# Layer 3 of a four-layer network: the head of the next chunk moved beside this chunk's stages, and local attention divided behind the context product

## The reference

```python
# between layers: x = x + s * g,  g = silu(ffn of the layer before);  xn = layernorm(x)
# L3 attention (16 heads of 8)
g = sigmoid(xn @ Wg + bg)                       # one gate a token
res = (1 - Z_I) * max(1 - Z_I - Z_J, 0) + Z_I * min(1 - Z_I + Z_J, 1)
scope = clip((s - 2) ** (1 - g) + 2 - |i - j|, 1e-32, 1)
probs = softmax(q k' / sqrt(8) + log(max(res * scope, 1e-32)))
s = probs @ v
# L3 feed-forward: two sub-layers (DEPTH = 2), each
#   local attention (8 heads of 64, windows of 64 looking one window back),
#   x = x + o @ wo;  then layer norm, w1, a * gelu(g), w2, x = x + ...
```

## Time and profile before

| | |
|---|---|
| median of three runs | 4228.34 us (4226.57 to 4237.04) |
| profiled execution, its own time | 4234.82 us |
| its span, first to last instruction | 4233.2 us |
| mean granted TensorE clock | 0.826 |
| busy: PE, PEld | 3121.1 us (74%), 1694.0 (40%) |
| busy: DVE, ACT, POOL | 2419.7 (57%), 1756.8 (42%), 1192.0 (28%) |

### The profile page before, as it was taken

One profiled execution on the slowest core, in us unless ns is written; L12 is line 12 of the kernel. 1 busy time (PEld: TensorE's weight loads), 2 busy tenths in 40 slices (PEclk: granted clock), 3 DMA queues, 4 the chain that ended last, 5 costly groups with the idle time before them and its releaser, 6 DMA issues. The chain is left out here.

```text
span 4233.2 us, 54691 instructions
## 1 busy us (share of the span) xinstructions
PE 3121.1 (74%) x20450; PEld 1694.0 (40%) x20450; DVE 2419.7 (57%) x3405; ACT 1756.8 (42%) x3556; POOL 1192.0 (28%) x878
## 2 busy tenths in 40 slices
PE   6788888887343778888767678676786867768687
PEld 3444444444131333444334344343443434434344
DVE  2344444444263778778855665556665565656655
ACT  2333333333132555556434434344343444535344
POOL 0000000000232454445543243332433324233242
PEclk7888888888655889999878879688796887969779
DMA  2000000000121222333300000000000000000001
GB/s 95 8 7 5 3 7 7 7 7 5 65 92 50 69 74 75 92 88 88 84 18 6 9 1 6 8 6 9 1 6 8 6 9 1 6 8 6 8 1 8
DMA packets 82171, 112.05 MB, mean 26 GB/s; under 512 B 9920, under 2 KB 47296, under 8 KB 81344
## 3 DMA queue, kind: packets, MB, share of 16 engines
q1 hardware_dynamic: 76608, 98.31, 7.7%
q0 software_dynamic: 5376, 11.02, 1.1%
HBM read 82.55 MB, written 26.74 MB: 26 GB/s over the span
## 5 line engine op out<-in xcount | busy, mean ns | idle before, releaser
L370 ACT ACTIVATE l_PT<-PB 128x512 f32<-128x512 f32 x512 | 277.9, 595 | 542.0 <-PE PB L281 542.0
L281 PE MATMUL PB<-l_QM,l_KP 32*128 32x256 f32 x2048 | 375.0, 496 | 131.6 <-DVE l_QM L419 76.0
L1412 POOL TENSOR_TENSOR l_ST<-l_ST,l_CT 128x1024 f32<-128x1024 f32 x128 | 316.4, 2472 | 354.3 <-DVE l_ST L1351 354.3
L408 DVE TENSOR_REDUCE keep_MXP<-PB 128x4 f32<-128x1024 f32 x256 | 301.3, 1219 | 109.1 <-PE PB L254 109.1
L1351 DVE TENSOR_TENSOR_SCAN l_ST<-l_DA,l_DB 128x1024 f32<-128x1024 f32 x128 | 355.6, 2778 | 4.4
L281 PEld LDWEIGHTS PB<-l_QM,l_KP 32*128 32x128 f32 x2048 | 242.7, 244 | 258.7 <-ACT l_PT L370 98.6
L704 POOL MEMSET l_KV<- 128x4 f32 x8 | 0.8, 104 | 941.3 <-POOLq L109 941.3
L1563 POOL TENSOR_TENSOR l_PT<-l_PT,l_PEN 128x512 f32<-128x512 f32 x168 | 213.1, 1290 | 186.0 <-ACT l_PT L370 186.0
L1345 DVE TENSOR_TENSOR l_DB<-PB,l_BT 128x1024 f32<-128x1024 f32 x128 | 155.3, 1213 | 137.5 <-PE PB L1111 137.5
L1274 ACT ACTIVATE l_DA<-PB,keep_aneg 128x510 f32<-128x510 f32 x256 | 161.1, 683 | 160.2 <-DVE l_ST L1351 83.4
L295 PE MATMUL PB<-l_PT,keep_VT 128*32 128x256 f32 x2048 | 187.6, 529 | 35.5 <-POOL l_PT L1563 25.6
(11 more groups left out here) (419 smaller groups left out, 6771.5 us busy)
## 6 DMA issues: line engine op xcount, KB each, us to landing
l_WB<-in_w2f_dram SPq DMA_DIRECT2D x80, 320.0 KB, 3.0
l_WB<-in_w2f_dram SPq DMA_DIRECT2D x80, 258.0 KB, 2.7
l_XR<-xs_mid SPq DMA_DIRECT2D x80, 64.0 KB, 1.8
ys_mid<-l_YO SPq DMA_DIRECT2D x80, 64.0 KB, 2.8
s_mid<-keep_S SPq DMA_DIRECT2D x17, 256.0 KB, 2.0
w3fs<-in_w3f_dram SPq DMA_DIRECT2D x1, 3127.0 KB, 18.1
keep_XI<-in_x_dram SPq DMA_DIRECT2D x9, 256.0 KB, 3.1
x_mid<-keep_X SPq DMA_DIRECT2D x9, 256.0 KB, 3.1
```

Of the source, the lines that this page charges most:

```text
L281: last = nc.tensor.matmul(PB[:, 4 + u % STBANKS, kt * SEQ:(kt + 1) * SEQ], b.KP[rows, a, i, k0:k0 + 128], b.QM[rows, n % 2, :], start=True ...
L370: nc.scalar.activation(b.PT[:, u % PSLOTS].rearrange("p k q -> p (k q)"), PB[:, 4 + u % STBANKS, :], ACT.Exp).then_inc(s.exp_done, 1)
L408: nc.vector.tensor_reduce(dst[:, 2 * pair:2 * pair + 2, :, 16 + n % 2], PB[:, 2 * pair:2 * pair + 2, :].rearrange("p r (t k) -> p r t k", ...
L1412: nc.gpsimd.tensor_tensor(b.ST[:, g % RING], b.ST[:, g % RING], b.CT[:, k % 2, :].unsqueeze(1).broadcast_to([128, 2, T]), ALU.mult).then_i ...
```

## The change

It does six things.

1. The head of a chunk's attention stage is done during the chunk before. Mixing (`gate_tokens`, now on POOL), turn, gate, residual, layer norm and gate logits run inside the attention stage, handed to PE, ScalarE and VectorE through a new argument `ahead`; the gate functions and the penalties run inside `layer3_ffn`, ten penalty steps and eight products on VectorE. Both penalty halves are VectorE's, written with other operations of the same value.
2. A new Block, `layer3_prepare`, does all of that once for the first chunk, in series, with the gather for the second.
3. Batch 0's multiplication by the penalties is shared like the others (three tiles on POOL).
4. In local attention the probabilities are no longer scaled. PE forms the row totals with two products by ones, and VectorE takes a reciprocal of 128x256 and multiplies the context by it. The loop is one step shorter; `G` and `HH` lie in the tile `CS`.
5. Loads, places and the two padding tiles reach one chunk further; the loads are issued at the start of `layer3_ffn`.
6. `att_tensor` issues `FIRST_MAX` = 11 fillers behind the first scores when there is no `ahead` (layer 0), and `NEXT_MAX` = 6 in layer 3. The two groups of fillers in layer 3's head go.

The diff, cut to its core:

```diff
+FIRST_MAX = 11
+NEXT_MAX = 6
+NEXT_TOKENS = 6
-def keep_warm(nc, c, PB, count=WARM):
+def keep_warm(nc, c, PB, count=WARM, bank=7):
@@ att_tensor
     scores(0)
+    if ahead:
+        ahead(0)
+    else:
+        keep_warm(nc, c, PB, FIRST_MAX)
...
             totals(0)
             if beside:
                 beside(0)
+            if ahead:
+                ahead(1)
...
+    if ahead:
+        ahead(2)
     values(BATCHES // 2 - 1)
     totals(1)
+    if ahead:
+        ahead(3)
@@ att_vector
-        for r in range(NR) if n == 0 else (NR - 1,):
+        u = NR * n + NR - 1
-        if masked and n == 0:
-            before(1)
-            weigh(0)
@@ layer 3, new functions
+def gate_products(nc, h, sq, link):
+    gates = slice(sq * SEQ, (sq + 1) * SEQ)
+    for t in (2 * sq, 2 * sq + 1):
+        nc.vector.scalar_tensor_tensor(out=h.T2[:, t, :], in0=h.AJ[:, gates], scalar=h.GI[:, t:t + 1], in1=h.GA[:, gates],
+                                       op0=ALU.add, op1=ALU.mult)
+        last = nc.vector.scalar_tensor_tensor(out=h.T1[:, t, :], in0=h.AJ[:, gates], scalar=h.NI[:, t:t + 1], in1=h.AJ[:, gates],
+                                              op0=ALU.add, op1=ALU.mult)
+    link(last)
...
+def penalty(nc, c, h, k, link):
+    sq, step = divmod(k, 5)
+    both, gates = slice(2 * sq, 2 * sq + 2), slice(sq * SEQ, (sq + 1) * SEQ)
+    two = lambda x: x[:, gates].unsqueeze(1).broadcast_to([128, 2, SEQ])
+    pen, t1, t2 = h.PEN[:, both], h.T1[:, both], h.T2[:, both]
+    if step == 0:
+        link(nc.vector.tensor_tensor(pen, c.dist.rearrange("p (t q) -> p t q", q=SEQ), two(h.PJ), ALU.add))
+    elif step == 1:
+        link(nc.vector.tensor_tensor(t2, t2, two(h.GA), ALU.min))
+    elif step == 2:
+        link(nc.vector.scalar_tensor_tensor(out=t1, in0=t1, scalar=0.0, in1=t2, op0=ALU.max, op1=ALU.add))
+    elif step == 3:
+        link(nc.vector.scalar_tensor_tensor(out=pen, in0=pen, scalar=1.0, in1=t1, op0=ALU.min, op1=ALU.mult))
+    else:
+        link(nc.vector.tensor_scalar(pen, pen, 1e-32, None, ALU.max))
@@ layer3_attention, PE
-                pe.wait_ge(s.y_mixed, 1)
...
-                keep_warm(nc, c, PB)
-                pe.wait_ge(s.x_gated, 1)
-                ln_tensor(nc, pe, s, c, c.X[:], PB)
-                keep_warm(nc, c, PB)
...
-                att_project(nc, pe, s, c, w, PB)
+                att_project(nc, pe, s, c._replace(XN=h.XN), w, PB)
+                def ahead(part):
+                    if part == 0:
+                        pe.wait_ge(s.y_gated, 1)
+                        turn_tokens(nc, c, PB, 7).then_inc(s.yT_ready, 1)
+                        pe.wait_ge(s.v_copied, 1)
+                        keep_warm(nc, c, PB, NEXT_MAX, 4)
+                        pe.wait_ge(s.y_copied, 1)
+                    elif part == 1:
+                        pe.wait_ge(s.x_ready, 1)
+                        nc.tensor.matmul(PB[:, 2, :], c.centre, h.X[:], start=True, stop=True).then_inc(s.ln_centred, 1)
+                    elif part == 2:
+                        pe.wait_ge(s.ln_square, 1)
+                        nc.tensor.matmul(PB[:, 3, :], c.mean, c.lnsq[:], start=True, stop=True).then_inc(s.ln_var, 1)
+                    else:
+                        pe.wait_ge(s.xn_ready, 1)
+                        ahead_gates(nc, h, w, PB).then_inc(s.gate_ready, 1)
@@ layer3_attention, ACT
+                def ahead(n):
+                    if n == 0:
+                        act.wait_ge(s.y_copied, 1)
+                        nc.scalar.activation(c.ga[:], c.Y[:], ACT.Abs).then_inc(s.ga_abs, 1)
+                    elif n == 1:
+                        act.wait_ge(s.ga_abs, 1)
+                        nc.scalar.activation(c.ga[:], c.ga[:], ACT.Exp, scale=-1.0).then_inc(s.ga_exp, 1)
+                    elif n == 2:
+                        act.wait_ge(s.ga_exp, 1)
+                        nc.scalar.activation(c.ga[:], c.ga[:], ACT.Ln, bias=c.one).then_inc(s.gate_log, 1)
+                    elif n == 4:
+                        act.wait_ge(s.gate_arg, 1)
+                        nc.scalar.activation(c.gb[:], c.gb[:], ACT.Exp).then_inc(s.gate_sigmoid, 1)
+                    elif n == BATCHES - 1:
+                        act.wait_ge(s.ln_centred, 1)
+                        nc.scalar.activation(c.lnsq[:], PB[:, 2, :], ACT.Square).then_inc(s.ln_square, 1)
+                    elif n == BATCHES:
+                        ahead_rstd(nc, act, s, c, PB)
@@ layer3_attention, DVE
+                def ahead(n):
+                    if n == 3:
+                        dve.wait_ge(s.gate_log, 1)
+                        nc.vector.scalar_tensor_tensor(out=c.gb[:], in0=c.Y[:], scalar=0.0, in1=c.ga[:], op0=ALU.min,
+                                                       op1=ALU.subtract).then_inc(s.gate_arg, 1)
+                    elif n == BATCHES:
+                        dve.wait_ge(s.kept, 2)
+                        ahead_norm(nc, dve, s, c, h, PB, link)
+                    elif n == BATCHES + 1:
+                        dve.wait_ge(s.gate_ready, 1)
+                        take_gates(nc, h, w, PB)
@@ layer3_attention, POOL
+                gate_tokens(nc.gpsimd, c, r, it + 1, link).then_inc(s.y_gated, 1)
+                nc.gpsimd.tensor_copy(c.X[:], h.X[:]).then_inc(s.kept, 1)
+                nc.gpsimd.tensor_copy(c.XN[:], h.XN[:]).then_inc(s.kept, 1)
+                pool.wait_ge(s.y_copied, 1)
+                nc.gpsimd.tensor_tensor(c.lnc[:], c.SI0[:], c.Y[:], ALU.mult).then_inc(s.product, 1)
+                for n in range(BATCHES):
+                    if n == NEXT_TOKENS:
+                        link(nc.gpsimd.tensor_tensor(c.lnc[:], c.lnc[:], c.gb[:], ALU.mult))
+                        pool.wait_ge(s.kept, 2)
+                        nc.gpsimd.tensor_tensor(h.X[:], c.X1[:], c.lnc[:], ALU.add).then_inc(s.x_ready, 1)
@@ layer3_ffn, PE
-                    for m in range(A + 4):
+                    for m in range(A + 3):
-                            pe.wait_ge(s.prob_ready, a0 + v + 1)
+                            pe.wait_ge(s.win_exped, a0 + v + 1)
+                            if v >= 2:
+                                pe.wait_ge(s.ctx_divided, a0 + v - 1)
+                            for h in range(2):
+                                last = nc.tensor.matmul(PB[LD * h:LD * h + LD, k, SEQ:2 * SEQ], c.ones[:, 0:LD],
+                                                        b.PT[:, v % 2, :].rearrange("p (w h q) -> p h w q", h=2, q=WIN)[:, h],
+                                                        start=True, stop=True, tile_position=(0, LD * h))
@@ layer3_ffn, ACT
+                    if l == 0:
+                        link(nc.scalar.activation(h.GU[:], h.GA[:], ACT.Abs))
+                        link(nc.scalar.activation(h.GU[:], h.GU[:], ACT.Exp, scale=-1.0))
                     for i in range(P):
+                        if l == 1 and i == 1:
+                            act.wait_ge(s.gu_ready, 1)
+                            gate_powers(nc, c, h, link).then_inc(s.gi_ready, 1)
...
+                    if l == 0:
+                        act.preload_act_table_set(LN)
+                        nc.scalar.activation(h.GU[:], h.GU[:], ACT.Ln, bias=c.one).then_inc(s.ga_logged, 1)
                     act.preload_act_table_set(EXP_LN)
@@ layer3_ffn, DVE
+                    if l == 1:
+                        dve.wait_ge(s.ga_logged, 1)
+                        gate_argument(nc, h).then_inc(s.gu_ready, 1)
...
+                        if l == 1 and i == 1:
+                            gate_negated(nc, h, link)
+                        elif l == 1 and i >= 2:
+                            gate_products(nc, h, i - 2, link)
...
+                    for m in range(A + 4):
+                        v = m - 4
+                        if 0 <= v:
+                            dve.wait_ge(s.ctx_ready, a0 + v + 1)
+                            link(nc.vector.reciprocal(b.RD[:], PB[:, 4 + 2 * (v % 2), SEQ:2 * SEQ]))
+                            nc.vector.tensor_tensor(b.OF[:, hp, sq * SEQ:(sq + 1) * SEQ], PB[:, 4 + 2 * (v % 2), 0:SEQ], b.RD[:],
+                                                    ALU.mult).then_inc(s.ctx_divided, 1)
...
-                            link(nc.vector.tensor_reduce(b.SM[:], b.PP[:, v % SCORES, :].rearrange("p (w k) -> p w k", k=128), AX.X, ALU.add))
-                            nc.vector.reciprocal(b.RS[:, v % SCORES, :], b.SM[:]).then_inc(s.win_recip, 1)
+                        if l == 1 and m in (2, 4, 6):
+                            penalty(nc, c, h, m // 2 - 1, link)
+                    if l == 1:
+                        for k in (3, 4, 5):
+                            penalty(nc, c, h, k, link)
                     dve.wait_ge(s.o_ready, l + 1)
...
+                        for k in (6, 7):
+                            penalty(nc, c, h, k, link)
                     ln_vector(nc, dve, s, c, b.HN[:], PB, link, l).then_inc(s.hn_ready, 1)
...
+                        for k in (8, 9):
```

(32 more changed lines are left out.)

279 lines of the change are left out of this document (151 added, 128 removed).

## The result

The changed kernel took 4056.16 us (median of 4 runs, 4048.41 to 4104.88) against 4227.45 for the kernel before on the same chip: a ratio of 0.9627, 95% interval 0.9542 to 0.9713. Faster by 171 us, where 230 was forecast. The profiled execution took 4052.55 us (span 4050.9, mean clock 0.876), 182.3 less span than before.

What follows compares the result with a forecast made beforehand. Waits between engines were taken to set the time, no engine being busy over three quarters of the span. 42 - 80 + 8 x (12 - 36) = -230 from the median of 4228.3 gave 3998 us, range 3925 to 4130.

Steps and rivals of the forecast that it cites:

- Part 5: Layer 0, behind the first scores: eleven fillers hold PE's clock through the wait for the first maxima, -80 us.
- Rival (c): Layers 0 and 3: the fillers do not hold the clock, giving 4136 us; chance 0.15.
- Part 4: New block before layer 3's loop: the first chunk's head done alone in series, +42 us once.
- Part 1: Layer 3's attention stage: head moved beside the chunk before, penalties ready for the second step, -36 us per chunk.
- The clock term of -5.3: Layer 3's later attention steps: half of 10.6 us per chunk, gained if PE's clock holds.
- Part 2: Second local-attention sub-layer: gates and penalties mostly fit idle time; negation and eight products cost +3.5 us per chunk.
- lie in a stretch where VectorE has hardly any idle: Second sub-layer: negation and eight products beside POOL's rotation cost 0.6 + 2 x 2.0 less about 1.1 us.
- Part 3: Layer 3's local attention: division behind the context product, +2.9 us in the first sub-layer, +5.7 in the second with penalties.
- (a): Local-attention division: slow reciprocal of 2.4 us makes VectorE set every step, +83, 4081 us; chance 0.10.
- (b): Local-attention division: cheap reciprocal of 0.42 us leaves PE bounding the loop, 3934 us; chance 0.15.
- (d): Layer 3's division becomes the bound; a reciprocal from 3.5 us loses the gain, 4.0 gives 4286 us; chance 0.03.
- counted as nothing: Layer 3's gather on POOL starts earlier, meeting the loop's middle; no cost, covered by POOL's freed 17 us.

Runs made afterwards that it cites:

- no_fill0: The changed kernel without the eleven fillers behind layer 0's first scores: 4085.73 us, ratio 0.97.
- after_again: The changed kernel once more, unaltered, in the second set of runs: 4027.74 us, ratio 0.9538.
- no_next: The changed kernel without the six fillers behind layer 3's first scores: 4148.51 us in one run.
- old_division: The changed kernel with local attention's old division (row sums, 128x4 reciprocal, GpSimd scaling) and the gather again behind the first loop: 3961.21 us, ratio 0.9437.
- old_division_behind: The changed kernel with the old division and the second sub-layer's products and penalties behind its loop: 3882.39 us, ratio 0.9209.
- after: The changed kernel as first measured and profiled, against the kernel before: 4056.16 us, ratio 0.9627.
- after_third: The changed kernel a third time, unaltered, in the third set of runs: 4077.69 us, ratio 0.9683.
- products_behind: The changed kernel with the second sub-layer's eight gate products and all ten penalty steps behind its attention loop: 3943.56 us, ratio 0.9384.

## Why the prediction was right, and where it was off

**Part 5** (-80): the mechanism is right where the clock holds, the size in part luck. Layers 0 to 2 lost 92.6 us in the first profile, 82 of it in the eight spans. But 26 of these 82 are the first chunk's, for which the forecast had put 25 down to the fillers, and no_fill0 had that short chunk without them. The fillers hold the clock in seven of eight chunks of the first profile and in four of eight in after_again; what the comparisons of no_fill0 with after_again show to be theirs lies between 39 us (the eight spans) and 58 (the medians), and in the first profile the other seven spans gave 56. Rival (c) is out as a whole, but the fillers hold in most chunks, not in all.

**Part 4** (+42): +40.6, from 17.0 to 57.5 us between the two markers.

**Part 1** (-36): -39.3, from two errors against each other. The first L436 comes at 14.4 us, not 10.8. I had allowed 2.2 us for slow projections; PE also starts 3.3 us late, as it does in every pass of the loop but the first (0.1 us there); the cause is not shown. The clock term of -5.3 was half of 10.6, for want of a reason to think that it would hold; in the first profile it holds in full, and the full term is about what no_next gives back (11.8 us). That the fillers were part of layer 3 too I had read in the diff and not priced.

**Part 2** (+3.5) is the first step that failed, within a forecast that held as a whole. I took 2.0 us for four products beside the rotation, with a credit of 1.1, as if VectorE's own time were all that counts. E's products and steps cost 7.9 to 9.0 where 3.5 + 2.8 were forecast; the eight products alone took 7.8 us of VectorE (four at 1.48, four at 0.47) where 2 x 2.0 stood. The step that failed is "lie in a stretch where VectorE has hardly any idle": it asked what they add to VectorE, and not who stands behind them in its queue, which was the last rotation and the first maxima, and behind those PE's clock.

**Part 3**, the division. The reciprocal was sized to 7 ns, closer than the working allowed: 153 and 256 x 6.4 ns give 1.79 us, out of which 1.75 was taken. The Trainium skill, "VectorE: DVE Perf Modes", section "First, the fixed hardware budget", gives the reciprocal a repeat count of 8, which read as eight cycles an element is an estimated 2.3 us. The row has 1757 ns, so here the measurement decides: (1757 - 153) / 256 is 6.3 ns, about six of the prediction's cycles of 1.04 ns. In the middle of C the divisions follow one another by 3.18 us (reciprocals at 3917.72, 3920.90 and 3924.08), forecast 3.15. The pairs of scores start less evenly than the 6.3 to 6.5 us of the forecast: 5.9, 6.6 and 6.4 us apart in C of five chunks of after_again, 5.9, 7.0 and 7.4 in the other three (before: 5.9, 5.5, 7.2), and 12.2, 7.9 and 6.2 in E of its last chunk, forecast 7. C without the stall is +2.4 us against +2.9, right. In E the division alone is +5.3 to +5.6 (old_division, old_division_behind) against +2.9, twice the size. The forecast gave this part no gain of its own and the runs give it none. With the products behind the loop, the old division is 9.8 us a chunk better in C and E (38.5 and 39.0 against 34.3 and 33.4) and 7.9 in the period (232.6 against 224.7): 61 us by the medians, 74 by the ratios. Rivals (a), (b) and (d) fell with the row.

**The gather** was "counted as nothing". It costs nothing in two sets (the first and the second), and 6 us a chunk, 48 in all, in the other three. That is the largest single miss of the first profile, in which layer 3's loop gained 8 x 7.7 = 62 us less than forecast. Its size is measured; what makes it come and go stays open.

So 4056 lies in the range by a sum whose largest terms were right in kind, of which the first chunk's 25 us were luck. Of the three things missed (products, division in E, gather), the products and the gather lay in waits of other engines, which no price of the added instruction itself shows. Why the division costs twice as much in E as in C was not separated.

## What to carry to other kernels

Before an instruction goes into a gap of an engine, name what is queued behind it there and which engine waits for that: eight products of 0.47 us put the first maximum off by 7.2 us. A change of several parts is worth taking apart on the chip even when it gains: here one part lost 61 to 74 us that the others hid. And put work that nobody waits for behind the loop, where VectorE waits for matmuls and for the output anyway: the ten penalty steps and eight products found room there, and F did not grow.

## What the runs showed that I had not expected

- The same single-core program stalls, or does not, from one set of runs to the next, in every chunk alike: C 38.1 or 44.1 us with the same instructions; the sets' medians are 4028 without the stall, 4056 and 4078 with it.
- Six identity matmuls behind the first scores decide the clock of a whole stage: 0.97 against 0.72 over 55 and 68 us.
- In layer 3's attention block PE starts 3.2 to 3.8 us after ScalarE's first instruction, on a wait of "issue", in every pass of the loop but the first, where it is 0.1 (after, after_again, after_third, products_behind).
- A VectorE scalar_tensor_tensor of 256 columns takes 0.47 us alone and 1.48 beside a GpSimd tensor_tensor of 512 columns.
